# Stacks of the split q and k through DRAM, groups spread over the batch, values last in a TensorE step

## The reference

```python
q = (x @ Wq).reshape(B, T, H, 2 * DH)      # B 8, T 512, H 16, DH 32
k = (x @ Wk).reshape(B, T, KV, 2 * DH)     # KV 4
v = (x @ Wv).reshape(B, T, KV, 2 * DH)
q1, q2 = q[..., :DH], q[..., DH:]          # k the same; rope on all four
a1 = softmax(q1 @ k1.T * scale + mask)
a2 = softmax(q2 @ k2.T * scale + mask)
out = (a1 - lam * a2) @ v                  # then a norm, @ Wo, x + ..., LayerNorm
```

## Time and profile before

| | us |
|---|---|
| median of the runs | 2554.3 |
| lowest and highest | 2542.62, 2565.25 |
| the profiled execution, its own time | 2561.59 |
| its span, from the first to the last instruction | 2559.7 |
| PE busy | 2112.7 (83%) |
| DVE busy | 1441.0 (56%) |
| ACT busy | 989.6 (39%) |
| POOL busy | 491.6 (19%) |
| mean granted TensorE clock | 0.87 of full speed |

### The profile page before, as it was taken

The page is one execution under the profiler, slowest core; times in us unless marked ns, Lnnn a source line. Parts: engine busy times, 40 slices in busy tenths (PEclk is TensorE's granted clock), DMA queues, the critical chain, the costliest instruction groups (busy, mean ns, idle before and its releaser), DMA issues. The chain is left out here.

```text
span 2559.7 us, 37845 instructions
## 1 busy us (share of the span) xinstructions
PE 2112.7 (83%) x10714; PEld 1537.0 (60%) x10715; DVE 1441.0 (56%) x3284; ACT 989.6 (39%) x2829; POOL 491.6 (19%) x452
## 2 busy tenths in 40 slices
PE   3778889889989889988898997987399999999900
PEld 2667756766866776776676686673255666666500
DVE  2577767777686686776877668552222222222256
ACT  1445545545454454554555555451011111111123
POOL 2122122211321322122231132110200000000065
PEclk7778889889789889988988988977599999999955
DMA  6734233432442433343343244210563222222178
GB/s 206 220 92 113 79 83 95 129 91 79 125 120 75 125 89 93 93 124 83 84 139 100 75 127 113 50 67 17 179 207 116 82 70 66 66 66 66 49 224 272
DMA packets 140274, 278.00 MB, mean 109 GB/s; under 512 B 29504, under 2 KB 38208, under 8 KB 137920
## 3 DMA queue, kind: packets, MB, share of 16 engines
q1 hardware_dynamic: 114240, 212.93, 29.9%
q0 software_dynamic: 10880, 35.66, 4.2%
q10 hardware_dynamic: 14976, 27.27, 2.8%
HBM read 132.09 MB, written 67.11 MB: 78 GB/s over the span
## 5 line engine op out<-in xcount | busy, mean ns | idle before, releaser
L713 ACT ACTIVATE expd<-S,neg_max 128x128 f32<-128x128 f32 (+3 forms) x1024 | 527.9, 526 | 250.1 <-DVE neg_max L814 247.7
L814 DVE TENSOR_REDUCE neg_max<-S 128x2 f32<-128x768 f32 (+3 forms) x384 | 399.6, 1041 | 379.0 <-PE S L557 378.8
L584 PE MATMUL O<-vals,probsT 128*128 128x64 f32 x2560 | 389.9, 299 | 129.7 <-DVE ctxn L859 129.2
L584 PEld LDWEIGHTS O<-vals,probsT 128*128 128x128 f32 x2560 | 375.3, 219 | 159.1 <-DVE ctxn L859 120.1
L555 PE MATMUL S<-kT,qT 128*128 128x256 f32 (+2 forms) x1024 | 416.3, 479 | 64.1 <-DMA qT<-parts 46.4
L723 ACT ACTIVATE probsT<-PTp 128x512 f32<-128x512 f32 (+2 forms) x384 | 202.3, 527 | 533.9 <-PE PTp L568 533.4
L845 DVE SCALAR_TENSOR_TENSOR mixed<-expd,rho 128x384 f32<-128x384 f32 (+3 forms) x512 | 346.2, 696 | 0.0
L555 PEld LDWEIGHTS S<-kT,qT 128*128 128x128 f32 x1024 | 229.4, 224 | 87.6 <-issue 49.4
L454 POOL TENSOR_TENSOR swapped<-swapped,rope_t 128x512 f32<-128x512 f32 x80 | 104.4, 1305 | 830.8 <-DVE swapped L801 830.8
L622 PE MATMUL tail<-wo,ctxT 128*128 128x512 f32 x512 | 256.5, 629 | 8.3 <-DVE ctxT L904 5.6
L568 PE MATMUL PTp<-ident,mixed 128*128 128x128 f32 x1280 | 236.7, 305 | 30.1 <-DVE mixed L845 26.4
(11 more groups left out here) (177 smaller groups left out, 2739.2 us busy)
## 6 DMA issues: line engine op xcount, KB each, us to landing
qT<-parts SPq DMA_DIRECT2D x1024, 64.0 KB, 2.0
wqk<-wqk_split SPq DMA_DIRECT2D x75, 512.0 KB, 3.8
xin<-expert_in_rows SPq DMA_DIRECT2D x72, 256.0 KB, 3.1
expert_out_rows<-yo ACTq DMA_DIRECT2D x72, 256.0 KB, 3.4
kT<-parts SPq DMA_DIRECT2D x256, 64.0 KB, 2.0
x<-in_x SPq DMA_DIRECT2D x8, 1024.0 KB, 5.4
x_rows<-x SPq DMA_DIRECT2D x8, 1024.0 KB, 5.4
out_y<-res ACTq DMA_DIRECT2D x32, 256.0 KB, 4.4
```

Source lines behind the costliest of these rows:

```text
L584: mm = nc.tensor.matmul(O[:, h, :], probsT[sl % 2][:, o:o + P], vals[kv][:, j, :], start=(j == 0), stop=(j == i))
L713: ex = nc.scalar.activation(expd[s % 3][:, k * slot:k * slot + w], S[s % 2][:, k * slot:k * slot + w], ACT.Exp, bias=neg_max[s % 3][:, k:k ...
L814: nc.vector.tensor_reduce(neg_max[s % 3][:, 0:k], v, AX, ALU.max, negate=True).then_inc(max_ready, 1)
```

## The change

It has four parts.

1. **Stack through DRAM.** `spread` stores the high part (128 by 512, 256 KB) and the low part in a DRAM tensor `parts_rows`, waits until both have landed, and loads them back in 4 DMAs of 32 partitions by 4 by 512 (256 KB each). The wait for the target to be free stands before the loads only.
2. **Groups spread.** `STARTS` counts steps of the batch. The starts were 1, 4, 12, 14, 16, 24, 26, 36, 38, 40 (v: 42, 44); now they are 0, 4, 8, 12, 16, 24, 27, 33, 36, 39 (v: 42, 44).
3. **PE's order within a step.** Part 1, tail work, part 0, and the values last.
4. **POOL.** Its body goes step by step. The scatter of a batch runs one batch later, one indirect DMA a step in steps 0 to 7. DVE's `high_part` waits for the stack first and for POOL second.

```diff
-STARTS = {0: {1: 0, 4: 1}, 1: {0: 2, 2: 3, 4: 4}, 2: {0: 5, 2: 6}, 3: {0: 7, 2: 8, 4: 9, 6: 10, 8: 11}}
-GROUP_BYTES = 256
+STARTS = {0: 0, 4: 1, 8: 2, 12: 3, 16: 4, 24: 5, 27: 6, 33: 7, 36: 8, 39: 9, 42: 10, 44: 11}
+GROUP_COUNT = 64
...
-            def spread(b, idx, kind, j, n, r2, free):
-                at_least(sp, scores_ready, free)
-                apart(sp)
+            def spread(kind, j, n, r2, total, free):
                 for side, done in ((0, hi_done), (1, lo_done)):
                     sp.wait_ge(done, n + 1)
                     apart(sp)
-                    for r in range(4):
...
-                        for k in blocks:
-                            sp.dma_start(dst[k * DH:(k + 1) * DH, :].bitcast(F32),
-                                         parts[r2][r * DH:(r + 1) * DH, side, :].bitcast(F32)).then_inc(stacked[r2], 16)
+                    sp.dma_start(parts_dram[r2, side], parts[r2][:, side, :].bitcast(F32)).then_inc(parts_out[r2], 16)
+                at_least(sp, scores_ready, free)
+                apart(sp)
+                sp.wait_ge(parts_out[r2], total // 2)
+                apart(sp)
+                for k in range(4):
+                    here = slice(k * DH, (k + 1) * DH)
...
+                    sp.dma_start(dst.bitcast(F32), parts_dram[r2, side].rearrange("(r p) t -> p r t", p=DH)) \
+                      .then_inc(stacked[r2], 16)
...
+            def body(b, first, second, last):
+                for s, kv, u in steps(b, first, last):
+                    for idx in fills(s, last, 1):
+                        if SEQ[idx][0] != "v":
+                            rope(group_no(b, idx), fill_no(b, idx), SEQ[idx][0])
+                    for idx in fills(s, last, 3):
+                        if SEQ[idx][0] != "v":
+                            low_part(group_no(b, idx), half(b, idx))
+                    if not first and not second:
+                        if s == 0:
+                            take_slots(b - 2)
+                        if s < NT * TOPK:
+                            scatter(s // TOPK, s % TOPK)
...
-                    for idx in fills(s, kv, last, 1):
+                    for idx in fills(s, last, 1):
                         fill_part(*SEQ[idx], 1, wqk[idx % 2][:], fill_no(b, idx))
-                    if lagged(b, s, LAG_V, first):
-                        values(*lagged(b, s, LAG_V, first))
-                    for idx in fills(s, kv, last, 0):
+                    if not first:
+                        for task in TAIL_PE.get(s, []):
+                            tail_task(b - 1, task)
+                    for idx in fills(s, last, 0):
...
                         fill_part(*SEQ[idx], 0, wqk[idx % 2][:], fill_no(b, idx))
-                    if not first:
-                        for task in TAIL_PE.get(s, []):
-                            tail_task(b - 1, task)
+                    if lagged(b, s, LAG_V, first):
+                        values(*lagged(b, s, LAG_V, first))
...
-            def high_part(n, r2, before):
+            def high_part(n, r2, total):
+                at_least(dve, stacked[r2], total)
+                apart(dve)
                 dve.wait_ge(rope_done, n + 1)
-                at_least(dve, stacked[r2], before)
```

More of the change, by code:

```diff
@@ L239, in attention_block @@
         lo_done = sem("lo_done")
+        parts_out = [sem(f"parts_out{r}") for r in range(2)]
         stacked = [sem(f"stacked{r}") for r in range(2)]
@@ L351, in lagged, with fills @@
             return (s - lag) % UB, b * UB + s - lag
-        def fills(s, kv, last, lag):
-            for start, idx in STARTS[kv].items():
-                if start == s % NU - lag and not (last and kv == KV - 1):
+        def fills(s, last, lag):
+            for start, idx in STARTS.items():
+                if start == s - lag and not (last and idx >= THIS_BATCH):
                     yield idx
@@ L421, in body @@
                 for idx, (kind, j) in enumerate(SEQ[:NGRP]):
-                    if last and idx >= 7:
+                    if last and idx >= THIS_BATCH:
                         continue
@@ L425, in body @@
                     apart(sp)
-                    if not (last and idx + 2 >= 7):
+                    if not (last and idx + 2 >= THIS_BATCH):
                         sp.dma_start(wqk[idx % 2][:].bitcast(F32), wsplit_dram[:, (idx + 2) % NGRP]).then_inc(w_in[idx % 2], 16)
@@ L449, in _, with take_vals @@
         def _(pool):
+            def take_vals(n, kv):
+                if not (isinstance(n, int) and n < KV):
+                    pool.wait_ge(ctx_full, (n - KV + 1) * NU)
+                apart(pool)
+                nc.gpsimd.tensor_copy(vals[kv][:], vnext[:, :, kv * HD:(kv + 1) * HD]).then_inc(vals_ready, 1)
             def rope(n, fill, kind):
@@ L505, in send, with scatter @@
                 apart(pool)
-                scatter(b)
-            def end(b):
-                send(b - 1)
+            def scatter(i, k):
+                nc.gpsimd.indirect_dma_start(
+                    xs_dram, bass.IndirectOffsetOnAxis(ap=idx[:, i, k:k + 1], axis=0), x1[:, i, :], None,
+                ).then_inc(scattered, 16)
+            def body(b, first, second, last):
[11 more added lines that the diff above has]
+                            scatter(s // TOPK, s % TOPK)
+                    if s == LAG_V + 1 and not first:
+                        take_vals(b * KV + KV - 1, KV - 1)
+                    if s >= UB - 2 and not last:
+                        pool.wait_ge(prep_out, fill_no(b, PER - 1))
+                        for k in range(KV - 1):
+                            if s == UB - 2 + k // 2:
+                                take_vals((b + 1) * KV + k, k)
+            def end(b):
+                for n in (b - 2, b - 1):
+                    take_slots(n)
+                    for i in range(NT):
+                        for k in range(TOPK):
+                            scatter(i, k)
                 pool.wait_ge(scattered, 16 * b * NT * TOPK)
@@ L518, in _ @@
                 take_vals(kv, kv)
-            batches(nc.gpsimd, body, end)
+            body(0, True, False, False)
+            body(1, False, True, False)
+            with nc.gpsimd.Fori(2, B - 1) as b:
+                body(b, False, False, False)
+            body(B - 1, False, False, True)
+            end(B)
         @block.tensor
```

66 lines of the change are left out of this document (20 added, 46 removed).

## The result

The changed kernel takes **2422.5 us**, the median of 4 runs (2416.4 to 2427.3), beside 2554.6 us for the kernel before in the same comparison. The ratio is 0.949, with a 95% interval from 0.946 to 0.952. The forecast was 2440 us.

The account below looks back on a forecast made before the run. PE was taken to set the pace, held up by waits for DVE at certain steps and by half clock. Gains of 73 + 30 - 5 + 20 = 118 us from 2561.6, less 7.3, gave 2440 us, range 2370 to 2532.

Parts of the forecast that it names:

- Values last (73 us): PE's waits for `ctxn` where a tile of rows begins: work put ahead hides about 97 of 129 us, 73 kept.
- The residue at `ctxn`: Waits left in a batch: 0.5 us at step 6, 1.9 at step 16, 2 at step 18, together 4.4 of 17.6.
- not all is kept: PE reaches the transposes sooner and waits there for DVE's mix: a quarter of the 97 us returns.
- the recorded sign for "wrong": PE's wait for DVE's mix before the transposes passing 80 us; it was expected at no more than 60, from 26.
- Stack (30 us): PE's waits for stacks: 22.0 us gone and 8 us saved at the start, with a chain of 10 us through DRAM.
- Starts (-5 us): Step 33's group needs the next batch's input earlier: costs 0.7 us a batch, 5 us over seven batches.
- POOL (0): Scatters moved into steps 0 to 7 fit between a rope and its low part: no effect on the time.
- Clock (20 us, bounds 0 and 71): Half-clock work after idle time at steps 16 and 18: about 6 of 42 us a batch recover, worth 20 us.
- The wait moves to the mix: Rival: three quarters of 97 us return before the transposes, clock does not recover; 2505, or 2530 at worst; chance 0.20.
- The clock recovers too: Rival: nothing returns and half of the half-clock time recovers, 71 us; about 2370 us; chance 0.14.
- The second hop comes late: Rival: stack chain of 35 us through full DMA queues, tightest at step 12, makes the kernel slower, 2595 us; chance 0.05.
- nothing changes: Rival: DVE and the DMA engines eat all of the gain, 2535 to 2560 us; chance 0.05.

Follow-up runs that it names:

- e1: Kernel before with only PE's order changed (part 1, tail work, part 0, values last); starts, stack and scatters as before: 2484.2 us.
- e2: Changed kernel with PE's old order within a step (part 1, values, part 0, tail work), the rest as changed: 2515.2 us.
- e6: Changed kernel with the scatters of a batch back in a row at the end of the next batch: 2424.7 us.
- e12: Changed kernel with each of POOL's three operations on a group issued as four of 128 columns, nothing left out: 2374.0 us.

## Why the prediction was right, and where it was not

The forecast of 2440 us missed by 18 us, a seventh of the gain, but it is the sum of terms whose errors cancel in part: the idle time was to lose 98 us and lost 78, and the clock was to give 20 and gave 67. That the total comes so near is in part luck.

**Values last (73 us).** The residue at `ctxn` came out right as a sum, 3.5 us a batch where 4.4 was forecast, and in part at other steps: step 18 still has about 2.3 us (forecast 2), steps 6 and 16 nothing (forecast 0.5 and 1.9), but step 12, which was to go, has 1.3 (at 1050.00 in batch 5). Alone the edit is worth 68 us, on top of the rest 93. The failed step is "not all is kept": the text let a quarter of the 97 us return before the transposes, because PE reaches them sooner. With the old starts (e1) about half of the 85 us return, but at several waits and only 6 us of them before the transposes. With the new ones almost nothing returns: from e2 to the changed kernel `ctxn` loses 55 us and PE's idle time 50, and the clock gives 48 more. What rose before the transposes, 54 us, rose without this edit, and the recorded sign for "wrong", over 80 us, is just reached (80.4). It comes with the new starts, which leave the step behind part 1 bare, and with POOL's instructions, which hold DVE there. The forecast looked at PE's order and at DVE's load, and at no place asked what DVE's durations depend on.

**Stack (30 us).** Right alone (30), and the chain, forecast at 10 us, took about 9. Its terms were off either way: the store was seen landed after 1.8 us, not 3.4, and the last load took 5.5, not 3.1, nearer to the forecast's upper case, in which four loads queue. The Trainium skill's formula, DMA: Bandwidth & Descriptors (Anatomy of one DMA, SWDGE path), made the chain an estimated 8.3 us. The trace is near it in the sum, but not in the hops, which the formula has at 2.6 us each. The formula is a fit of DMAs that GpSimd issues, and SP issues these. First scores came at 56.4 us, a little past the 54 to 56. No wait for a stack is left in batches 1 to 7. On top of the other parts it is worth only 11 us, since the starts had already taken those waits.

**Starts (-5 us).** The term had only the cost of the next input, and that did not come: PE waits for `xl` nowhere in the middle batches. What the starts bring was counted under values last (the half groups ahead of the waits), and nothing of it for the stack. Alone they are worth 30 us, on top of the rest 18. So the sign of the term was wrong.

**POOL (0).** Right: e6 is at 2424.7 against 2422.5.

**Clock (20 us, bounds 0 and 71).** Mis-sized: the same matmuls took 67 us less. In the six middle batches it is 35 us, 5.9 a batch. At 0.45 us for each microsecond at half clock, that is 13 us a batch that rose to full clock, where the text took 6. It had let only the stretch behind steps 16 and 18 recover, and in batch 5 that stretch did give back 7 us of half clock. The rest of that batch's 10 us is mostly at step 8 and at the change of batches, and the text had held the latter fixed. Ahead of and behind the six batches the term had 4 us, and it was 32. The runs bear the link out: PE's busy time falls with the idle time, from 2112.7 to 2083.0 (e1) and 2045.6 us (after) and to 2017.0 in e12.

**The middle batch** of 190 to 195 us at clock 0.92 was 194.4 at 0.92.

**The rivals.** "The wait moves to the mix" has its wait in the trace, 54 us of the 73 that it had, but from another cause, and it did not hold back the clock. "The clock recovers too" was met in part: its 71 us stand for 9.5 a batch, and the middle batches gave 5.9; the 67 come near it only with the start and the end. "The second hop comes late" did not happen (the chain is 9 us and not 33), and neither did "nothing changes".

## What to carry to other kernels

When work is spread evenly over steps, look at what the old bunching covered: a step that loses its fill work shows every lateness of the engine behind it. Read the longest and the shortest duration of one instruction form before an engine's load is taken as given; a form that takes twice its time may be standing for another engine, which a kernel without that engine's work can tell, and cutting the other's instructions shorter may be worth more than the reordering. Parts of a change that take away the same wait don't add up, so price each with the others in place.

## What the runs showed of the hardware

- Some instructions of DVE stood until an instruction of POOL was over: a mixture 1.58 us in place of 0.73, a ratio 1.24 in place of 0.21, a TENSOR_SCALAR of 128 by 512 0.91 in the mean in place of 0.54. Batch-norm statistics of 128 by 512 did not (0.68 in both). Over the kernel it was 140 us of DVE's 1439. That 247 us of POOL's busy time cost the kernel 92 us, on an engine busy for a fifth of the span, was not expected.
- POOL's operation on 128 by 128 took 0.49 to 0.54 us in the mean and on 128 by 512 about 1.3 to 1.5, so quarters cost it 134 us more in all. The kernel still gained 48 us.
- A store of 256 KB to DRAM was seen landed 1.8 us after its issue, and a load of 256 KB into 32 partitions, four in a row, took 4.4 to 4.7 us in the median and 5.5 for the last of one group, while loads of the same size into `xin` took 3.1.
